# A one-core transformer block: f32 projections as f16 pairs, feed-forward in units of 256 tokens, the first q by batch, low halves on GpSimd, and a new order

## The reference

```python
xn = _layernorm(x, axis=-1)
x = x + _L0_attn_ref(xn, L0_attn_Wqkv, L0_attn_Wo) + _L0_ffn_ref(xn, L0_ffn_A, L0_ffn_B, L0_ffn_Wr)
xn = _layernorm(x, axis=-1)
x = x + _L1_attn_ref(xn, L1_attn_Wq, ...) + _L1_ffn_ref(xn, L1_ffn_gate_wq, ...)
# first layer's attention, for each batch:
scores = where(causal, einsum('bqhd,bkd->bhqk', q, k) * scale + alibi, NEG_INF)
attn = einsum('bhqk,bkd->bqhd', softmax(scores), v) @ Wo
# second layer's feed-forward:
h = silu(x @ gate.T) * (x @ up.T);  out = h @ down.T
```

## Time and profile before

| | us |
|---|---|
| median of three runs (lowest, highest) | 666.8 (666.42, 670.37) |
| the profiled execution, its time | 666.2 |
| its span, first to last instruction | 664.4 |
| mean granted TensorE clock, share of full speed | 0.969 |

### The profile page before, as it was taken

How to read it: one execution, slowest core, us unless ns; L and a number is a source line. 1 busy time by engine, 2 the same in 40 slices (tenths; PEclk the granted TensorE clock), 3 DMA queues, 4 the chain that set the end, 5 groups by cost and what they waited for, 6 DMA issues and landing times.

```text
span 664.4 us, 11736 instructions
## 1 busy us (share of the span) xinstructions
PE 620.2 (93%) x4490; PEld 359.8 (54%) x4490; DVE 454.2 (68%) x936; ACT 349.8 (53%) x603; POOL 284.2 (43%) x299
## 2 busy tenths in 40 slices
PE   5989566978999999999999999999999999999997
PEld 4464444545665565565655755574654555454443
DVE  5775598984988987674668966686796554457422
ACT  3220696682558965843448748852684772023310
POOL 4203476550319773521315826632357561016310
PEclk9998685998999999999999999999999999999999
...
DMA packets 34567, 34.78 MB, mean 52 GB/s; under 512 B 8816, under 2 KB 24080, under 8 KB 34512
## 3 DMA queue, kind: packets, MB, share of 16 engines
...
## 4 chain that ended last, share of the span: by engine, by line
PE 78%; DVE 8%; ACT 5%; issue 4%; DMA 3%; SPq 1%; POOL 0%; ACTq 0%; DVEq 0%
PE B_bank L1014 28%; PE B_bank L1035 14%; PE A_bank L983 10%; PE A_bank L900 5%; PE B_bank L922 5%; PE A_bank L954 4%; PE E_bank L938 3%; ACT probs L810 2%; DVE mx L1225 2%; ACT e L809 2%; PE A_bank L869 2%; PE B_bank L900 2%; PE E_bank L934 2%; DMA q_parts<-qs 1%; PE B_bank L1004 1%
## 5 line engine op out<-in xcount | busy, mean ns | idle before, releaser
L733 POOL TENSOR_TENSOR probs<-e,probs 128x512 f16<-128x512 f32 x128 | 153.8, 1208 | 189.4 <-ACT probs L810 179.7
L1014 PE MATMUL B_bank<-xs,wgu 128*128 128x512 f16 x896 | 200.5, 379 | 0.0
L809 ACT ACTIVATE e<-E_bank,wn 128x512 f32<-128x512 f32 x192 | 135.6, 706 | 100.1 <-PE E_bank L938 52.5
L1014 PEld LDWEIGHTS B_bank<-xs,wgu 128*128 128x128 f16 x896 | 85.4, 98 | 96.3
L810 ACT ACTIVATE probs<-E_bank,wn 128x512 f16<-128x512 f32 x192 | 135.6, 706 | 0.0
L1035 PE MATMUL B_bank<-wd,hbuf 128*128 128x512 f16 x448 | 100.3, 379 | 0.0
L1225 DVE TENSOR_REDUCE mx<-B_bank 128x8 f32<-128x256 f32 (+6 forms) x168 | 87.5, 584 | 7.2 <-PE B_bank L922 7.1
L745 POOL TENSOR_TENSOR hbuf<-hf,hbuf 128x512 f16<-128x512 f32 x56 | 67.7, 1215 | 43.7 <-ACT hbuf L836 43.6
L983 PE MATMUL A_bank<-wo_sb,attnT 128*128 128x512 f32 x160 | 71.1, 594 | 0.0
L922 PE MATMUL B_bank<-kk,qq 128*128 128x32 f16 (+20 forms) x512 | 67.4, 269 | 3.5 <-DVE mx L1225 3.2
L1035 PEld LDWEIGHTS B_bank<-wd,hbuf 128*128 128x128 f16 x448 | 43.4, 98 | 48.3
...
## 6 DMA issues: line engine op xcount, KB each, us to landing
...
```

The lines of the kernel that those rows point to most:

```text
L733: pool.tensor_tensor(probs[:, u % PSLOTS, 1, :], e32[:, w, :], probs[:, u % PSLOTS, 0, :], ALU.subtract).then_inc(s_lo01, 1)
L809: act.activation(e32[:, w, :], psum("exp", i, g, w)[:, :], ACT.Exp, scale=wn[:, 7:8])
L1014: mm = pe.matmul(psum(name, c, i)[:, :].rearrange("p (t n) -> p t n", t=NT), wgu[:, m, k, i * P:(i + 1) * P], xs[:, :, part, k, :], start= ...
```

## The change

- **f16 pairs.** The products with Wq and the token weights in chunks 1 to 3, and with Wo in all batches, are no longer f32. Weights and tokens are each split into a high and a low f16 part, and three f16 products (`PAIRS`: high-high, high-low, low-high) stand for one f32 product; the LoRA rows have two. Chunk 0's q and tok stay f32.
- **Preparing the weights.** `hi` on ScalarE writes the high part and a scaled f32 copy (four times for Wq, once for the token weights, five times for Wo), `lo` on GpSimd subtracts them. `squares2`, `norm2` and `scale2` find the scales. Wo and the LoRA rows are loaded earlier.
- **Low halves of turned tiles.** After ScalarE's high copy, VectorE writes a low half for `xT0` (chunks 1 to 3) and for `attT`. `midT` turns the LoRA middle in f16.
- **First q by batch.** In chunk 0, q is made in halves of 256 columns, `q0(b, m)`, batch 0 first, and stored by batch.
- **Units of 256 tokens.** The second layer runs over 8 units u (one batch each) instead of 4 chunks. A gate or up step takes two tiles of the inner width with 256 columns each: 16 products of 256 columns. ScalarE's tanh and VectorE's up product come as two halves of 256. S, m1 and den1 have two copies. A down tile is cut into `half`, `half2`, `half3`, `down` for the order.
- **Low halves of probabilities.** GpSimd makes w = 2 too from batch 2 on (`LOWS = 2`).
- **Token rows.** For batch 1 they come by a transfer of 1 MB on SyncE's queue (`hot_rows`), not by four VectorE copies. `setup2` moves from VectorE to GpSimd.
- **Order.** New costs, and a new table of ranks with a third number for the first chunk.

```diff
+def low_by(i, w):
+
+    return "DVE" if w == 2 and i < LOWS else "POOL"
+
+
+UNITS = [(i, g, w) for i in range(2 * NCH) for g in range(NHG) for w in range(3)]
+LOW_COUNT = {}
+for _e in ("DVE", "POOL"):
+    for _n, _u in enumerate([u for u in UNITS if low_by(u[0], u[2]) == _e]):
+        LOW_COUNT[_u] = _n + 1
+
+
 def lows(i, g, w):
 
-    return [dve("exp", i, g, 2)] if w == 2 else [pool("exp", i, g, w)]
+    return [dve("exp", i, g, w)] if low_by(i, w) == "DVE" else [pool("exp", i, g, w)]
 
...
+    for k in range(2):
+        p.add("PE", ("attT", i, k), dve("pv", i, NHG - 1), *([pe("out", i - 1, 1, gap=0.0)] if i else []))
         p.add("ACT", ("attT", i, k), pe("attT", i, k), *([pe("out", i - 1, 1)] if i else []))
+        p.add("DVE", ("attT", i, k), act("attT", i, k))
...
+        p.add("PE", ("outa", i, t), sp("x1_load", 2 * i + t, gap=0.0), dve("attT", i, 0), dve("attT", i, 1), act("midT", i),
+              *([pool("lo", 9), pool("clear")] if i == 0 else []))
+        p.add("PE", ("out", i, t), pe("outa", i, t, gap=0.0))
...
+    for n in range(2 * NK if c == 0 else 0):
+        b, m = n // NK, n % NK
+        p.add("PE", ("q0", b, m), act("xT0", 0, 2 * b), act("xT0", 0, 2 * b + 1), at=9.0 + m)
+        p.add("ACT", ("q0", b, m), pe("q0", b, m), dve("scale"), *([("ACT", ("store", b, m - 2), 2.5)] if m > 1 else []))
+        p.add("DVE", ("q0", b, m), act("q0", b, m))
+        p.add("ACT", ("store", b, m), dve("q0", b, m))
...
+    for i in range(NPR):
+        first = [dve("xT1", u, t) for t in range(NU)] + ([pe("down", u - 2, NU - 1)] if u > 1 else [])
+        if u == 0:
+            first += [pool("ffn_load", N_FFN - 1, gap=10.0)]
...
+            for n in range(10):
+                p.add("ACT", ("hi", n), dve("scale") if n < NK else dve("scale2", 0 if n == NK else 1))
+                p.add("POOL", ("lo", n), act("hi", n))
             p.add("DVE", ("setup0",), pool("late", 1, gap=6.0))
-            p.add("DVE", ("setup1",), pool("late", 10, gap=8.0), dve("nm", 0))
+            p.add("DVE", ("setup1",), pool("late", 11, gap=8.0), dve("nm", 0))
...
+            def hot_rows():
+                sp.wait_ge(s_hotrow, 1)
+                sp.dma_start(qq[R_HOT:P, 1, :, :], hot.unsqueeze(1).broadcast_to([P - R_HOT, NH, SEQ])).then_inc(s_hot[1], 16)
...
+            def lo(n):
+                pool.wait_ge(s_whi, n + 1)
+                if n < NK:
+                    low, scaled, high = wq2[:, n, 1, :], wq_scaled[:, n, :], wq2[:, n, 0, :]
+                elif n == NK:
...
-                    pool.wait_ge(s_gather[1], 16 * 3)
-                if n == 4:
+                if n == 5:
                     pool.wait_ge(s_nmrow[0], 32)
+                    pool.wait_ge(s_wlo, NK + 1)
...
+            def hi(n):
+                act.wait_ge(s_sw, 1) if n < NK else act.wait_ge(s_scale2, 1 if n == NK else 2)
+                if n < NK:
+                    act.activation(wq2[:, n, 0, :], wq_sb[:, n, :], ACT.Identity, scale=wm[:, 15:16])
+                    last = act.activation(wq_scaled[:, n, :], wq_sb[:, n, :], ACT.Identity, scale=wm[:, 15:16])
...
+                        wait_used(pe, "xT0", 0, t)
+                wait_free(pe, "q0", b, m)
+                for k in range(NK):
+                    mm = pe.matmul(psum("q0", b, m)[:, 0:SEQ].rearrange("p (t n) -> p t n", t=2), wq_sb[:, k, m * P:(m + 1) * P],
...
+            def q_tiles(c, m, ks):
+                for k in ks:
+                    for n, (wpart, xpart) in enumerate(PAIRS):
+                        mm = pe.matmul(psum("q", c, m)[:, :].rearrange("p (t n) -> p t n", t=NT), wq2[:, k, wpart, m * P:(m + 1) * P],
+                                       xp[:, :, xpart, k, :], start=(k == 0 and n == 0), stop=(k == NK - 1 and n == 2))
...
-                pe.wait_ge(s_lo01, 2 * (n + 1))
-                pe.wait_ge(s_lo2, n + 1)
+                for w in ((1, 2) if low_by(i, 2) == "DVE" else (2,)):
+                    wait_low(pe, i, g, w)
...
+            def out_tiles(i, t, ks):
+                for k in ks:
+                    for n, (apart, wpart) in enumerate(PAIRS if k < NK else PAIRS[0:2]):
+                        tokens = attnT[:, apart, k, t * P:(t + 1) * P] if k < NK else midT[:, t * P:(t + 1) * P]
+                        mm = pe.matmul(psum("out", i, t)[:, :], tokens, wo2[:, k, wpart, :],
+                                       start=(k == 0 and n == 0), stop=(k == NK and n == 1))
...
+            def gate_or_up(name, u, i, m):
+                t0 = NU * u % NT
+                wait_free(pe, name, u, i)
+                for a in range(2):
+                    for k in range(NK):
+                        for part in (0, 1):
+                            mm = pe.matmul(psum(name, u, i)[:, a * SEQ:(a + 1) * SEQ].rearrange("p (t n) -> p t n", t=NU),
+                                           wgu[:, m, k, (2 * i + a) * P:(2 * i + a + 1) * P], xs[:, t0:t0 + NU, part, k, :],
+                                           start=(k == 0 and part == 0), stop=(k == NK - 1 and part == 1))
+                mm.then_inc(full(name, u, i), 1)
...
+                dve.wait_ge(s_xTh, NT * (c - 1) + t + 1)
+                dve.scalar_tensor_tensor(out=xp[:, t, 1, :, :].rearrange("p k n -> p (k n)"), in0=psum("xT0", c, t)[:, :], scalar=XS,
+                                         in1=xp[:, t, 0, :, :].rearrange("p k n -> p (k n)"), op0=ALU.mult,
+                                         op1=ALU.subtract).then_inc(free("xT0", c, t), 1)
+
...
+                for a in range(2):
+                    cols = slice(a * SEQ, (a + 1) * SEQ)
+                    h = dve.scalar_tensor_tensor(out=hf[:, n % 2, cols], in0=psum("up", u, i)[:, cols],
+                                                 scalar=sux[:, 2 * i + a:2 * i + a + 1], in1=hf[:, n % 2, cols],
+                                                 op0=ALU.mult, op1=ALU.mult)
+                h.then_inc(free("up", u, i), 1)
```

893 lines of the change are left out of this document (529 added, 364 removed), and 17 rows, old and new, of tables (RANK, US).

## The result

| | before | changed |
|---|---|---|
| median of four runs (lowest, highest), us | 667.29 (666.42, 670.37) | 639.01 (638.76, 639.22) |
| span of the profiled execution | 664.4 | 636.9 |
| granted TensorE clock, mean | 0.969 | 0.958 |

The ratio is 0.9574, with a 95% interval of 0.9543 to 0.9606: the changed kernel is 4.3% faster. The forecast was 629, with a range of 612 to 648.

The account below looks back on a forecast made before the run. Bound: TensorE's work, plus a start of about 120 us in which it is not full. Span 664.4 - 35 - 1 - 5 + 3 = 626.4 us; the median lies 2.4 above the span, so 629 us, range 612 to 648.

Parts of the forecast that it names:

- What bounds the kernel: Whole kernel: TensorE's work, gapless from 190 us, plus a start of about 120 us in which it is not full.
- TensorE's work: All TensorE products: output projection saves 20.5, q tiles 10.4, token products 4.2; sum 35 us less (30 to 37).
- gate and up: Second layer: 896 matmuls of 512 columns become 1,792 of 256 with own weight loads, at a cost of 0.
- The rival of exposed loads: Gate and up: doubled weight loads not hidden behind matmuls, slower than before, 717 to 805 us; chance 0.03.
- the first output tile at about 115: Start: first output tile at 115 instead of 120.7 us; idle and slow time up to there -1 (-10 to +10).
- The code loads: GpSimd's start: loads around the all-reduce, 5.3 and 5.3 to 9.5 us, letting max reductions begin at 42 to 46.
- `nm` comes 3 us later, near 60: Max stretch on VectorE: 10.53 us plus low halves of x (3) and a scale chain (3) delay `nm`.
- end near 67 and are not last: Start: ScalarE's five pairs of Wo copies end near 67 us, with GpSimd's first low half at 70.
- From 121 to 190: Feed-forward of unit 0 starts near 125 and fills gaps; idle 6.3 falls to 1.3, -5 us (-6 to -2).
- The steady part: Full stretches: low halves hidden on GpSimd, but a static order leaks more with less TensorE work, +3 us (0 to +12).
- The start is lost: Rival: first exponential delayed by 10 more, or the leak is 12 instead of 3; 640 to 650 us; chance 0.17.
- the forecast's own case: Whole kernel: time of 616 to 640 us, around the forecast of 629; chance 0.63.

Follow-up runs that it names:

- e11: Changed kernel with the fourth product (low by low) added in the output projection and q of chunks 1 to 3, 112 matmuls more: 660.6 us.
- e10: Changed kernel with one of three products left out in the output projection and q of chunks 1 to 3, 112 matmuls fewer: 632.6 us.
- e8: Kernel before, with gate and up products computed in halves of 256 columns, each matmul with its own weight load: 670.3 us, ratio 1.0039 to 1.0086.
- e2: Changed kernel with GpSimd's all-reduce moved behind the low half of the token weights: 642.6 us.
- e3: Changed kernel with SyncE's 1 MB transfer of the second batch's token rows moved behind the first gather: 640.5 us.
- e4: Changed kernel with three moves together: Wo's squares behind the turned copies, all-reduce behind the low halves, token rows behind the first gather: 644.3 us.
- e1: Changed kernel with ScalarE's sum of squares of Wo put behind the last turned copy of x: 637.5 us.
- e5: Changed kernel with Wo's squares and the token rows moved later and GpSimd's low halves, ln0, all-reduce and Wo issues reordered: 637.2 us.
- e7: Changed kernel with the 48 low halves of probabilities (third batch on) moved from GpSimd back to VectorE: 645.5 us.

## Why the prediction was right, and where it missed

**What bounds the kernel.** Right for this change: e11 shows that going back towards the kernel before costs most of the added work. The prediction's reason, that the full stretches are gapless, was enough for that, but it wouldn't have been for more: e10.

**TensorE's work.** 35 forecast, 32.5 measured as busy time, which also holds the lower clock of the start (0.78 for 0.81 from 20 to 121 us, 0.95 for 0.98 from 121 to 190). The output tile took 3.02 (6.04/2), a q tile 2.59, as worked out from the earlier trace rows. The token products were 24 at 44.6 ns (1.07 us to the next product, from 342.20), as taken. The mis-sized term is gate and up: forecast 0, measured 1.7 by the chain and 2.4 by e8. The rival of exposed loads is dead; the reading of the earlier trace rows, that a load hides behind a matmul, was right.

**Idle time up to the first output tile.** This is the step that failed: "the first output tile at about 115". It came at 129.0, past the 125 that the prediction itself had named as a sign of being wrong. Forecast -1 for idle and slow time, measured +6 of idle time from 20 to 121, and a clock of 0.78 instead of 0.81. Its parts:

- The code loads came where the prediction put them, 5.65 and 7.57 us, and the max reductions at 46.4, at the edge of its 42 to 46. The reason it gave was only half of it: without the loads ahead they still began at 45.5 (e2), with the loads but without the slow store at 45.4 (e3), and without either at 38.3 (e4).
- What the loads did hold is a chain of which the prediction gave only the end (the copies of Wo): Wo is issued behind them (47.2), so its squares begin at 55.9 and the scale ends at 65.8.
- "`nm` comes 3 us later, near 60": it came at 66.4. The max stretch held the four low halves of x, but two of them waited 3.36 us for ScalarE, where the squares of Wo waited for the transfer. The prediction didn't name what was queued behind that wait. Its own terms for the stretch add up to 16.5 us (10.53 + 3 + 3). It lasted 20.0, and 16.3 in e1, where the wait is gone: the work was priced rightly, the wait was missing. Most of the rest of the 6.4 is the start of the max reductions, 2.4 behind the middle of 42 to 46.
- ScalarE's copies of Wo were to "end near 67 and are not last": they ended at 72.2, because the scale chain ended at 65.8. With e5 taken as a check, the first low half then depends on GpSimd's issues as well.
- From 85 to 125 us VectorE and ScalarE seem to set the pace, which the forecast treated as a shift of a block. e5 began it 5.4 us earlier and the tile came 1.9 earlier (not told from no shift); e4 began it 7.0 later and the tile came 5.7 later.

**From 121 to 190.** Forecast -5, measured -1.6: the gate rows started at 150.6 and not near 125. Of these 26 us, 14 are the late tile; the others lie between the tile and the gate rows, and weren't followed. Of the 4.7 us of idle time left, 2.2 lie ahead of the mark.

**The steady part.** Forecast +3, measured +0.8 of idle time after 190. e7 tells that the term hangs on how the work is shared: with VectorE carrying the 48 low halves the time would have been some 5 us more. The leak that the prediction spoke of does come with less work in the same order: 4.9 us of idle time more in e10. The prediction had called these low halves hidden on GpSimd, which was right, and had not asked what they cost on VectorE.

**Rivals.** "The start is lost" described the start well (it asked for the first exponential 10 us later, it was 7 later than before and the low half 6 later than forecast), but the time stayed in the forecast's own case, 616 to 640, because behind the tile things went 3.5 us better than forecast. That is luck as far as the start goes: the forecast had the tile 6 us earlier than before, it came 8 later, and only the other terms and the width of the case took that in.
